# A vision tower on one core: leaving out matmuls whose results nobody reads

## The reference, cut to what matters

```
x = coords @ fc0_w + fc0_b                       # 3 -> 32 channels
for sw, cw, cb in four layers:
    x_ft = rfft2(x)[:, :, :20, :20]              # 20 x 20 modes are kept
    out  = einsum("bixy,ioxy->boxy", x_ft, sw)   # mixes channels, mode by mode
    x1   = irfft2(out padded with zeros)
    x2   = einsum("bchw,oc->bohw", x, cw) + cb   # pointwise
    x    = gelu(x1 + x2)
h = gelu(x @ fc1_w + fc1_b) @ fc2_w + fc2_b      # 32 -> 64 -> 1: a 64 x 64 map an image
h = concat(cls_tok, h)                           # 65 tokens of width 64
h = h + attention(layernorm(h))                  # QKV projections, 8 heads, band of +-32
h = h + lattice_ffn(layernorm(h))                # top 6 of 64 experts
```

## Time and profile before

| | us |
|---|---|
| median of three runs | 1089.97 |
| the profiled execution's own time | 1089.02 |
| its span, first to last instruction | 1086.0 |
| PE busy | 996.6 (92%) |
| DVE busy | 618.7 (57%) |
| ACT busy | 410.1 (38%) |
| mean granted TensorE clock | 0.979 of full speed |

### The profile page before, as it was taken

One profiled execution on the slowest core, in us unless ns is written; L12 is line 12 of the kernel. 1 busy time (PEld: TensorE's weight loads), 2 busy tenths in 40 slices (PEclk: granted clock), 3 DMA queues, 4 the chain that ended last, 5 costly groups with the idle time before them and its releaser, 6 DMA issues.

```text
span 1086.0 us, 36279 instructions
## 1 busy us (share of the span) xinstructions
PE 996.6 (92%) x16844; PEld 620.2 (57%) x16844; DVE 618.7 (57%) x773; ACT 410.1 (38%) x554; POOL 155.2 (14%) x159
## 2 busy tenths in 40 slices
PE   4899899999989998999999899999999999589996
PEld 3567567656657533676576567656126888522221
DVE  2278357637734222576378358542254677779887
ACT  2332233323223495332232233324767787321100
POOL 6000000000000000000000000120011764234411
PEclk9999999999999899999999999999899999689999
DMA  5220230031023102300320220020010000000000
GB/s 194 93 78 3 78 94 2 5 116 54 3 93 121 36 6 73 85 20 4 105 66 3 94 77 3 17 94 2 13 21 36 2 1 1 2 1 1 1 10 10
DMA packets 25916, 46.71 MB, mean 43 GB/s; under 512 B 9949, under 2 KB 11000, under 8 KB 25125
## 3 DMA queue, kind: packets, MB, share of 16 engines
q1 hardware_dynamic: 24118, 42.47, 12.7%
q0 software_dynamic: 1456, 1.60, 0.5%
q10 hardware_dynamic: 192, 0.33, 0.1%
HBM read 30.21 MB, written 10.89 MB: 38 GB/s over the span
## 4 chain that ended last, share of the span: by engine, by line
PE 75%; DVE 12%; issue 6%; ACT 4%; POOL 2%; DMA 1%; SPq 0%; POOLq 0%; DVEq 0%
PE PSALL L1298 22%; PE PSALL L1266 7%; PE PSALL L1160 5%; PE PSALL L1289 5%; PE PSALL L1375 5%; PE PSALL L1241 4%; PE PSALL L1174 4%; PE PSALL L526 3%; PE PSALL L1385 3%; DVE WORK L1505 3%; PE PSALL L429 3%; DVE WORK L1524 2%; DVE WORK L1005 2%; PE PSALL L514 2%; PE PSALL L1285 2%
## 5 line engine op out<-in xcount | busy, mean ns | idle before, releaser
L1524 DVE STREAM_TRANSPOSE WORK<-PSALL 128x1024 f32<-128x1024 f32 x128 | 152.4, 1229 | 249.6 <-PE PSALL L1266 249.6
L1298 PEld LDWEIGHTS PSALL<-EW,WORK 128*64 128x64 f32 x4096 | 221.8, 138 | 72.7 <-issue 48.3
L1298 PE MATMUL PSALL<-EW,WORK 128*64 128x128 f32 x4096 | 247.6, 276 | 14.0 <-DVE WORK L1524 13.7
L1424 ACT ACTIVATE X<-PSALL,TABLES 128x1024 f32<-128x1024 f32 x128 | 141.9, 1115 | 306.7 <-PE PSALL L1298 306.7
L1505 DVE STREAM_TRANSPOSE WORK<-PSALL 128x1024 f32<-128x1024 f32 x84 | 104.3, 1241 | 32.7 <-PE PSALL L1160 30.9
L325 POOL DMA_DIRECT2D WORK<-MIXED x32 | 17.9, 560 | 667.1 <-ACT MIXED L1415 553.8
L1406 ACT COPY SPEC<-PSALL 128x400 f32<-128x400 f32 x64 | 53.8, 850 | 135.7 <-PE PSALL L1174 132.8
L1174 PEld LDWEIGHTS PSALL<-TABLES,WORK 128*64 128x64 f32 x2000 | 67.0, 138 | 48.9 <-DVE WORK L1505 31.4
L1005 DVE TENSOR_TENSOR WORK<-PSALL,X 128x832 f32<-128x832 f32 x80 | 79.7, 1018 | 19.2 <-PE PSALL L514 18.0
L1174 PE MATMUL PSALL<-TABLES,WORK 128*64 128x64 f32 x2000 | 80.7, 228 | 8.0 <-DVE WORK L1505 3.8
L1458 ACT ACTIVATE WORK<-PSALL,B 128x1024 f32<-128x1024 f32 x64 | 68.0, 1111 | 20.9 <-PE PSALL L1375 20.6
(11 more groups left out here) (158 smaller groups left out, 1154.7 us busy)
## 6 DMA issues: line engine op xcount, KB each, us to landing
SW<-in_spec_w SPq DMA_DIRECT2D x160, 80.0 KB, 2.7
spec_scr<-MIXED SPq DMA_DIRECT2D x24, 400.0 KB, 3.3
SPEC<-spec_scr SPq DMA_DIRECT2D x32, 200.0 KB
WORK<-spec_scr SPq DMA_DIRECT2D x16, 200.0 KB
WORK<-in_coords_w SPq DMA_DIRECT2D x2, 1024.0 KB, 4.9
XC<-in_coords_c SPq DMA_DIRECT2D x2, 1024.0 KB, 7.2
WORK<-MIXED SPq DMA_DIRECT2D x40, 40.0 KB
WORK<-MIXED POOLq DMA_DIRECT2D x32, 40.0 KB
```

The source lines that it names most:

```text
L1298: m = pe.matmul(PS[2 * p + z][64 * j:64 * j + 64, 2 * b * GRID:(2 * b + 2) * GRID], G[:, n % 2, b, h:h + 2, :, t].rearrange("p q o -> p (q ...
L1424: nc.scalar.activation(X[:, n].rearrange("p b (z d) c w -> p d z b (c w)", z=2)[:, p, :, :, 2 * t * GRID:2 * (t + 1) * GRID], PSALL[:, 2 * ...
L1524: nc.vector.transpose(G[:, n % 2, 2 * x + y].rearrange("p h o v -> p o h v"), PSALL[:, 4 + 2 * x:6 + 2 * x, :].rearrange("p k (h o v) -> p ...
```

## The change

The six products ahead of the QKV part and the two in each layer run's wait are left out, with the function `keep_busy`. Nothing is added and nothing else is moved: PE, which ran them before it came to the wait behind them, now comes to that wait directly. In all, 2 x 8 + 6 = 22 matmuls go (44 matmul records), and no other engine's program differs.

```
@@ tail_tensor
-            for i in range(6):
-                pe.matmul(PS[7], ident[:], TABLES[:, :, 0:128], start=True, stop=True)
             for c in range(NC + 2):
                 if c < NC:
                     pe.wait_ge(y_ready, c * BC // LB + 1)
@@ tensor
-            def keep_busy(count):
-
-                for i in range(count):
-                    pe.matmul(PS[4], ident[:], work[:, 0:BANK], start=True, stop=True)
-
             def layer(p, l):
...
                 mix()
                 pointwise(l, 0, 0)
-                keep_busy(2)
                 inverse_rows(l, 0, 0)
```

## The result

The changed kernel takes 1118.73 us (median of four runs, 1111.98 to 1120.86) against 1089.03 us before: ratio 1.0263, 95% interval 1.0238 to 1.0288. It is slower, as forecast, but by 29.7 us and not by 10, and outside the stated range (1092 to 1110). The profiled execution took 1117.26 us.

The account below looks back on a forecast made before the run. PE time and its clock were taken to bound the kernel almost everywhere. From 1089.02 us, 11.6 for layer clock falls and a net -1.7 at QKV (-3.08 + 1.4) gave 1098.9, taken as 1099 us; range 1092 to 1110.

Parts of the forecast that it names:

- The sixteen products are hidden; direct gain 0.: Eight layer waits: the next instruction waits for mode copies, not the unread products, so removing them directly gains 0 us.
- The clock falls in each wait or just behind it.: Layer runs: idle gaps of 2.20 and 1.36 us around 1.31 us of work bring PE to half clock.
- the clock stays up: Rival for the whole kernel: no clock fall, only the 3.08 us at QKV count, 1085.9 us; chance 0.05.
- only the long gap counts: Rival: a single gap decides, layers keep full clock and only QKV falls, 1087.3 us; chance 0.06.
- half of the runs fall: Rival: the clock falls in about half of the runs, 1093.1 us; chance 0.12.
- The price of a fall: 1.1 us short, 2.5 us long, three short ones to one long.: Behind each layer wait: half-clock loss averaging 1.45 us a run, 11.6 us over eight.
- 3.08 us are gained at QKV.: Start of QKV: without the six products the transposes follow the first layer norm and start 3.08 us earlier.
- One short slow stretch with QKV work in it, 1.4 us.: Start of QKV, after 3.69 us of idle PE: half clock for 3.3 us, costing 1.4 us.
- a rival, at 11.9 us: QKV part: clock stays low for all 18.10 us, losing 11.9 us, total 1109.4; chance 0.15 shared with long layer falls.
- long falls in all layers: Rival for the eight layer runs: every fall is long, 20 us, total 1107.3; chance 0.15 shared with slow QKV.
- My last sign of being wrong: QKV part: the prediction is wrong if the slow stretch there reaches to the scores.
- The range.: Whole kernel time: 1092 to 1110 us, meant to leave out no more than 0.2 of the chance.

## Why the prediction was wrong

Point by point, in its own order.

- *The sixteen products are hidden; direct gain 0.* Right: L1264 starts after the same 2.20 us in the run shown, and the trace now names the mode copies as what it waits for.
- *The clock falls in each wait or just behind it.* Right: eight of eight, in the changed kernel and with the layers' products alone left out. The rivals in which the clock stays up, in which only the long gap counts, and in which half of the runs fall, all fell: gaps of 2.20 and 1.36 us around 1.31 us of work were enough. The advice of the Trainium skill (TensorE: Matmul & The Clock Gate, "Why this matters for your kernels") on single long gaps fits the QKV start, 4.01 us of idle PE, and not the layers.
- *The price of a fall: 1.1 us short, 2.5 us long, three short ones to one long.* The prices were near (1.35 and about 2.1, with 1.9 and 2.6 for two other long ones); the mix was wrong: six of eight were long. The reason that I gave for short ones, that the work there uses more rows of the array and soon runs without a pause, did not hold. The term was 11.6 us; it measured 14.1 in the profile and 13.4 as a kernel of its own, both with what the dense layers' own falls gave or took.
- *3.08 us are gained at QKV.* Right but for 0.33: it was 2.75 us. Of what is missing, 0.15 is the hand-over from DVE, and by the rest the first layer norm came later behind the last fc2 products.
- *One short slow stretch with QKV work in it, 1.4 us.* **This is the step that failed.** The stretch lasted 40.8 us and cost 15.6. I had it as a rival, at 11.9 us and a chance of 0.15 shared with long falls in all layers, and argued against it from one fall, at 835, that ended after 3.3 us. I had placed that fall in the QKV part's last chunk, and that was a misreading: the scores start at 834.56, so it began and ended in their sixteen 128 x 128 products, and said nothing of QKV work. The long stretch here also ends in the scores, 4.4 us behind their start. In a chunk such products are mixed with small ones. That the clock stays low for this reason is argued and not shown; what is shown is that it stays low through all eight chunks and that six dense products in the middle bring it back. The evidence for the rival stood in my own rows: at 371 and 763.4 the clock stayed low in work that kept PE busy all the time, and from 934 on for 23.8 us, a stretch that my list of lengths left out. The price per chunk was low too: I took a factor of 1.68 from one group of eight small matmuls; the chunks went from 2.35 to 4.38 us, 1.86. My last sign of being wrong, a slow stretch that reaches the scores, is what came.
- *The range.* It took long layer falls and a slow QKV part as alternatives. They hang on the same doubt, whether busy PE brings the clock back soon, and came together: with six long falls and two short ones at my prices and QKV at 1.86 the sum is 1089.0 + 17.2 - 3.1 + 15.1 = 1118.2 us. That this is so near the measured 1118.7 is partly luck, for its term of the layers is 3 us above the 14.1 measured.

What stays open: why a fall in the layers is long in one run and short in another. The mix differs between executions (six and two, five and three), and the times of the kernels that have falls spread over 3 to 9 us. Also open is why the dense layers bring a fall in one execution and none in another.

## What to carry to other kernels

A matmul that nobody reads can be worth keeping: before it is removed, see whether it fills a wait (then removing it gains nothing directly) and what the granted clock does without it. Ask of each part behind a wait not only whether the clock falls, but what there would raise it again; a long part made mostly of small matmuls can stay at half clock to its end. And such filling belongs ahead of a wait whose end it does not delay: moved there, and added to three more waits, it made this kernel 0.6% faster in all.

## What the runs showed of the hardware that I had not expected

- The same work goes on at either level. The QKV chunks run at 2.4 GHz for 18 us when they start there (1.00 in 813.90 to 832.00) and at 1.2 GHz for 40.8 us when they start there, with PE busy 39.69 of 40.80 us.
- Six dense products of 128 x 128 by 128 x 512 raised the clock in the middle of that part; taking 7.65 us themselves, they paid for it by the medians (1097.64 against 1101.37 us).
